# Second convolution of a fused network on four 32-column strips, and three whole-image passes on ScalarE

## The chip, the cores and the metric

The kernel runs on 1 core of one Trainium2 chip. The metric is the device time of one execution in microseconds. In this text PE is TensorE, DVE is VectorE, ACT is ScalarE, POOL is GpSimd and SP is SyncE, which only issues transfers; ACTq and SPq are the sequencers of ACT and SP while they issue one.

## What is computed

The input is 64 images of 16 channels of 128x128, float32. Four layers each add a function of the group-normalised image (8 groups of 2 channels) to the image:

```python
x = x + _L0_conv_ref(_gn(x), 5)      # Newton-Schulz inverse of each 128x128 channel, 5 iterations
x = x + _L1_conv_ref(_gn(x), L1_conv_weight_int8, L1_conv_scale_weight, L1_conv_bias)  # 8-bit 3x3
x = x + _L2_conv_ref(_gn(x), L2_conv_filter_w)
x = x + _L3_conv_ref(_gn(x), L3_conv_weight)   # 3x3 with circular borders
```

Layer 1 quantises its input with one step for the whole batch, `round(clip(x / scale_input, -127, 127))`. Layer 2 is a 5x5 convolution whose kernel is zero off its diagonal:

```python
kernel = filter_w[..., :, None] * jnp.eye(k, dtype=filter_w.dtype)   # k = 5, padding 2
```

So tap d reads the pixel d rows down and d columns to the right, d = -2 .. 2, and there are five taps and not 25.

## The kernel before

The program has two blocks. The first does the inverse of layer 0 for all images, and ends near 2272 us. The second does layers 1 to 3, and everything that the prediction speaks of lies there.

**Layout.** An image stands in SBUF as 128 partitions by 2048 elements. A partition is (row within a band of 8, channel), and the free dimension is (16 bands, 128 columns). Four bands make a chunk of 512 columns, one PSUM bank, so each layer has four chunks u = 0 .. 3. A convolution is a sum of matmuls of a 128x128 weight matrix (all rows and channels of a band to all rows and channels of a band) with a chunk shifted sideways, and one "halo" matmul with 96 partitions, for the input rows that lie in the neighbouring band. Those 6 rows x 16 channels are copied from the normalised image `xn` into the tile `xh` by six transfers of one row each, three issued by ACT (line 1184) and three by SP (line 1130). Layers 2 and 3 use float16 in two parts, a high part and the remainder, and so every weight matrix costs three products; layer 1 needs one.

**Normalisation.** For layers 2 and 3 DVE computes scale and mean in small columns (lines 1312 to 1320) and the scaled image F over 2048 elements (line 1322). ACT rounds F to float16 (`upper`, line 1202), POOL subtracts that from F (`lower`, line 1164, four instructions), and then the image counts as normalised (`normed`). For layer 1 DVE makes three passes over the image (`quantise`, lines 1243, 1246, 1248). In layer 3 ACT also copies the circular borders (`wrap`, lines 1192 to 1197), and then issues the halo transfers.

**Order.** The code is written out by hand as steps, and each engine has its own fixed order and waits on semaphores. PE's step s is layer 1 of image s, layer 2 of image s-1 and layer 3 of image s-2. The tiny matmuls `mean` and `var` of the next statistics stand between their chunks. The order on ACT in step s, with waits, is this:

```python
def step(s, h, odd):
    if there(s - 2):
        wrap(s - 2, odd)
        act.wait_ge(wrapped, 2 * s - 2)
        halos(3, s - 2, odd)
    if there(s):
        root(2, s)
        upper(2, s, odd)
    if there(s + 1):
        first(s + 1, h + odd, 1 - odd)
    if there(s):
        act.wait_ge(normed[2], s + 1)
        halos(2, s, odd)
    if there(s - 1):
        root(3, s - 1)
        upper(3, s - 1, 1 - odd)
```

`first` issues the halo transfers of layer 1 and adds the bias to the whole image (line 1214). `root` is the square root of a column (line 1207), which DVE waits for before its columns of lines 1312 to 1320.

Of the kernel before, what the change touches and what calls it, by code (L numbers as in the profile page):

```python
# [19 lines left out]
H = 128  # L20
C = 16
G = 8
CPG = C // G
RB = 8
NJ = H // RB
PW = H + 4
L = 2
# [6 lines left out]
WUP = 2.0 ** 14  # L34
# [7 lines left out]
def conv_net(nc, x, ident, gmat, gsel, w1, w1h, w2, w2h, w3, w3h, scale_w, bias, x1d, out):  # L42
# [32 lines left out]

    def images(step, first, last, turn):

        for i in range(first, last):
            step(i, i // turn, i % turn)

    keep = ExitStack()
    with keep:
# [19 lines left out]
        sws = persistent("sws", [H, 1])  # L102
        banks = [keep.enter_context(nc.psum_tensor(f"bank{n}", [H, 512], f32)) for n in range(8)]
# [3 lines left out]
        taps = (None, 3, 5, 3)  # L107
        kinds = (None, bf16, f16, f16)
# [3 lines left out]
        wt = [None] + [persistent(f"wt{l}", [H, parts[l], taps[l], H], kinds[l]) for l in (1, 2, 3)]  # L112
        wth = [None] + [persistent(f"wth{l}", [6 * C, parts[l], H], kinds[l]) for l in (1, 2, 3)]
        wf = [None] + [persistent(f"wf{l}", [H, taps[l], H]) for l in (1, 2, 3)]
        whf = [None] + [persistent(f"whf{l}", [6 * C, H]) for l in (1, 2, 3)]
# [9 lines left out]
        w_loaded = sem("w_loaded")  # L125
        w_top = sem("w_top")
# [11 lines left out]
        with mem:  # L138
# [103 lines left out]
            with nc.Block() as block:  # L242

                @block.sync
                def _(sp):
# [17 lines left out]
                    for l, body, rows in ((1, w1, w1h), (2, w2, w2h), (3, w3, w3h)):  # L263
                        sp.dma_start(wf[l][:, :, :], body).then_inc(w_loaded, 16)
                        sp.dma_start(whf[l][:, :], rows).then_inc(w_loaded, 16)
                    for i in range(A_FIRST):
                        step(i, i // SLOTS, i % SLOTS)
# [11 lines left out]
                def _(pool):  # L279
                    nc.gpsimd.memset(ones[:, :], 1.0).then_inc(ones_set, 1)  # L280
                    nc.gpsimd.memset(onesm[:, :], 1.0 / (2 * H)).then_inc(ones_set, 1)
                    nc.gpsimd.memset(onesv[:, :], 1.0 / (CPG * H * H)).then_inc(ones_set, 1)

# [144 lines left out]
                def _(act):  # L428
# [45 lines left out]
                    def upper_weights(l):  # L474

                        if l == 1:
                            act.wait_ge(w_loaded, 16 * 6)
                        else:
                            act.wait_ge(w_chain, 6 * (l - 1))
                        nc.scalar.activation(wt[l][:, 0, :, :], wf[l][:, :, :], ACT.Copy).then_inc(w_high, 1)  # L480
                        nc.scalar.activation(wth[l][:, 0, :], whf[l][:, :], ACT.Copy).then_inc(w_high, 1)
# [81 lines left out]
                def _(dve):  # L563
# [120 lines left out]
                    def weight_rows(l):  # L684

                        if l == 2:
                            dve.wait_ge(w_loaded, 16 * 6)
# [3 lines left out]
                    def weight_top(l):  # L691

                        w = wtop[l]
                        link = Link(dve, w_chain, 6 * (l - 2))
# [5 lines left out]
                    def weight_scale(l):  # L700

                        w = wtop[l]
                        link = Link(dve, w_chain, 6 * (l - 2) + 2)
                        dve.wait_ge(w_top_all, l - 1)
                        link.done(nc.vector.tensor_copy(w["s"][:, :], banks[7][:, H - 4 + l:H - 3 + l]))
                        link.wait()
                        link.done(nc.vector.reciprocal(w["i"][:, :], w["s"][:, :]))
                        link.wait()
                        link.done(nc.vector.tensor_scalar(wf[l][:, :, :], wf[l][:, :, :], w["i"][:, 0:1], WUP,
                                                          ALU.mult, ALU.mult))  # L710
                        link.done(nc.vector.tensor_scalar(whf[l][:, :], whf[l][:, :], w["i"][0:6 * C, 0:1], WUP,
# [4 lines left out]
                    def lower_weights(l):  # L716
                        dve.wait_ge(w_high, 2 * l)
                        nc.vector.tensor_tensor(wt[l][:, 1, :, :], wf[l][:, :, :], wt[l][:, 0, :, :],
                                                ALU.subtract).then_inc(w_split, 1)
                        nc.vector.tensor_tensor(wth[l][:, 1, :], whf[l][:, :], wth[l][:, 0, :],  # L720
                                                ALU.subtract).then_inc(w_split, 1)
# [124 lines left out]
                    link.wait()  # L846
                    dve.wait_ge(pads_zeroed, 6)
# [3 lines left out]
                def _(pe):  # L851
# [66 lines left out]
                    def weight_broadcast(l):  # L918
                        pe.wait_ge(w_chain, 6 * (l - 2) + 2)
# [579 lines left out]
```

## Time and profile before

| what | value |
|---|---|
| time, median of 3 runs | 4286.94 us (4285.88 to 4287.16) |
| span of the profiled execution | 4285.7 us, 1.2 us under the median |
| PE busy | 4194.6 us, 98% of the span |
| DVE busy | 3444.2 us, 80% |
| POOL busy | 2407.9 us, 56% |
| ACT busy | 2072.5 us, 48% |

The busy shares are means over both blocks. In the second block, which starts at about 2272 us, PE is at its limit and ACT and POOL are a quarter busy. ACT's busy time leaves out the time in which its sequencer issues transfers. Beginnings and ends of matmuls overlap in the trace, so the spacing of their starts says what one costs.

### The profile page before, as it was taken

What the parts mean: (1) busy time and instruction counts of PE and PEld (TensorE: products, weight loads), DVE (VectorE), ACT (ScalarE), POOL (GpSimd) and SP (SyncE); (2) the same over time, 40 slices, a digit from 0 to 9 for tenths busy, and PEclk for the clock granted to TensorE, in tenths of its full rate; (3) what the DMA queues carried; (4) which work ended last, traced back from release to release, by engine and by line L of the source; (5) the groups of instructions that cost most, each with busy time, mean ns of one, the idle gap of its engine ahead of it and who ended that gap; (6) DMA issues with size and microseconds to landing.
All of it is one profiled execution on the core that took longest, in us unless ns stands there. A gap on an engine that the chain in (4) does not pass through costs nothing. (4 is left out here: it accounts for less than half of the span.)

```text
span 4285.7 us, 81705 instructions
## 1 busy us (share of the span) xinstructions
PE 4194.6 (98%) x30409; PEld 3108.7 (73%) x30409; DVE 3444.2 (80%) x7393; ACT 2072.5 (48%) x4296; POOL 2407.9 (56%) x3149
## 2 busy tenths in 40 slices
PE   7999999999999999999996999999999999999998
PEld 7999999999999999999992444444444444444443
DVE  6888888888888888888876787878787888888784
ACT  5776777777777777777761222222222222222221
POOL 6888888888888888888871222222222222222221
PEclk9999999999999999999997999999999999999999
DMA  2221222222222222222214555555555555555553
GB/s 69 64 62 55 65 65 60 60 60 60 60 66 65 60 63 68 60 60 60 60 41 97 133 137 134 137 133 137 134 138 134 138 134 138 134 138 134 138 134 84
DMA packets 333657, 404.28 MB, mean 94 GB/s; under 512 B 23088, under 2 KB 286032, under 8 KB 316880
## 3 DMA queue, kind: packets, MB, share of 16 engines
q1 hardware_dynamic: 308688, 334.25, 30.8%
q10 hardware_dynamic: 24576, 64.79, 5.6%
q8 instruction: 246, 4.03, 0.4%
q14 instruction: 147, 1.20, 0.1%
HBM read 135.22 MB, written 134.22 MB: 63 GB/s over the span
## 5 line engine op out<-in xcount | busy, mean ns | idle before, releaser
L1392 PE MATMUL bank<-xn,wt 128*128 128x512 f16 (+1 forms) x6912 | 1661.6, 381 | 19.9 <-issue 10.7
L1164 POOL TENSOR_TENSOR xn<-F,xn 128x512 f16<-128x512 f32 x512 | 541.6, 1090 | 1453.2 <-ACT xn L1202 1453.2
L1392 PEld LDWEIGHTS bank<-xn,wt 128*128 128x128 f16 (+1 forms) x6912 | 672.9, 100 | 805.0 <-issue 21.9
L463 ACT ACTIVATE P<-bank 128x512 f32<-128x512 f32 x1024 | 606.8, 608 | 264.0 <-PE bank L962 154.5
L1266 DVE SCALAR_TENSOR_TENSOR x<-bank,wu,x 128x512 f32<-128x512 f32 x512 | 382.4, 747 | 313.7 <-PE bank L1399 306.6
L1202 ACT ACTIVATE xn<-F 128x2048 f16<-128x2048 f32 x128 | 244.9, 1913 | 603.3 <-DVE F L1322 603.3
L1399 PE MATMUL bank<-xh,wth 96*128 96x512 f16 (+1 forms) x1792 | 515.6, 380 | 12.1 <-DMA xh<-xn 12.1
L313 POOL TENSOR_TENSOR W<-W 128x512 f16<-128x512 f32 x256 | 290.3, 1166 | 145.7 <-ACT W L489 145.7
L1277 DVE BATCH_NORM_STATS2 bs<-x 128x6 f32<-128x512 f32 x512 | 355.6, 695 | 17.7
L569 DVE BATCH_NORM_STATS2 st<-X 128x6 f32<-128x256 f32 x1024 | 351.5, 411 | 5.8 <-DMA X<-in_x 5.7
L1399 PEld LDWEIGHTS bank<-xh,wth 96*128 96x128 f16 (+1 forms) x1792 | 174.2, 97 | 232.6 <-DMA xh<-xn 15.7
L358 POOL TENSOR_TENSOR S<-P 128x512 f32<-128x512 f32 x256 | 317.8, 1272 | 32.0 <-ACT P L463 31.6
L369 POOL TENSOR_TENSOR P<-P,idt 128x512 f32<-128x512 f32 x256 | 318.4, 1278 | 29.0 <-ACT P L463 28.8
L353 POOL TENSOR_TENSOR YX<-idt,YX 128x512 f32<-128x512 f32 x256 | 324.1, 1278 | 5.5 <-ACT YX L453 5.5
L498 ACT ACTIVATE W<-X,nb,r 128x256 f32<-128x256 f32 x512 | 259.4, 590 | 134.2 <-POOL nb L341 130.7
L1207 ACT ACTIVATE sd<-ve 128x1 f32<-128x1 f32 x128 | 26.1, 204 | 608.9 <-DVE ve L1303 603.0
L364 POOL TENSOR_TENSOR S<-S,P 128x512 f32<-128x512 f32 x256 | 318.1, 1274 | 0.0
L453 ACT ACTIVATE YX<-bank,cs 128x128 f32<-128x128 f32 x1024 | 277.7, 381 | 11.8 <-PE bank L894 3.5
L673 DVE SCALAR_TENSOR_TENSOR X<-bank,cout,X 128x128 f32<-128x128 f32 x1024 | 270.5, 344 | 12.9 <-PE bank L988 12.9
L607 DVE TENSOR_TENSOR P<-bank,idt 128x512 f32<-128x512 f32 x256 | 177.0, 692 | 109.0 <-PE bank L979 103.2
L929 PE MATMUL bank<-YX 128*128 128x128 f32 x2048 | 260.9, 276 | 0.0
L944 PE MATMUL bank<-P 128*128 128x128 f32 x2048 | 260.2, 277 | 0.0
(129 smaller groups left out, 7619.3 us busy)
## 6 DMA issues: line engine op xcount, KB each, us to landing
X<-in_x SPq DMA_DIRECT2D x64, 1024.0 KB, 4.8
x_scratch<-X SPq DMA_DIRECT2D x64, 1024.0 KB, 5.6
X<-x_scratch SPq DMA_DIRECT2D x64, 1024.0 KB, 8.8
out<-x SPq DMA_DIRECT2D x64, 1024.0 KB, 3.9
xh<-xn SPq DMA_DIRECT2D x384, 131.8 KB, 4.5
xh<-xn ACTq DMA_DIRECT2D x384, 131.8 KB, 5.4
xh<-xn SPq DMA_DIRECT2D x192, 65.9 KB, 3.2
xh<-xn ACTq DMA_DIRECT2D x192, 65.9 KB, 2.7
```

Source lines behind the costliest of these rows:

```text
L313: nc.gpsimd.tensor_tensor(W16[:, 1, at, :], W[:, at, :], W16[:, 0, at, :], ALU.subtract).then_inc(w_lower, 1)
L353: nc.gpsimd.tensor_tensor(e, eyes, e, ALU.subtract).then_inc(a_new, 1)
L358: nc.gpsimd.tensor_tensor(quad(S, q), quad(P1, q), quad(P2, q), ALU.add).then_inc(s_new, 1)
L364: nc.gpsimd.tensor_tensor(quad(S, q), quad(S, q), quad(P3, q), ALU.add).then_inc(q_new, 1)
L369: nc.gpsimd.tensor_tensor(quad(P2, q), quad(P2, q), eyes, ALU.add).then_inc(r_new, 1)
L463: nc.scalar.activation(into[:, 4 * q:4 * q + 4, :], banks[q][:, :].rearrange("p (m w) -> p m w", m=4), ACT.Copy).then_inc(sb, 1)
L569: ins = nc.vector.bn_stats((st0, st1)[k][:, g, :], group_of(X[slot], g))
L1164: ins = nc.gpsimd.tensor_tensor(padded(xn[l][odd], 1)[:, a + 1:a + 5, L:L + H], F[l][:, a:a + 4, :], padded(xn[l][odd], 0)[:, a + 1:a + 5, ...
L1266: nc.vector.scalar_tensor_tensor(out=dst, in0=bank, scalar=wtop[l]["u"][:, 0:1], in1=xs[l][odd][:, a:b, :], op0=ALU.mult, op1=ALU.add).the ...
L1277: nc.vector.bn_stats(bst_[l][:, u, :], xs[l][odd][:, 4 * u:4 * u + 4, :]).then_inc(gchain[l], 1)
L1392: nc.tensor.matmul(bank, wt[l][:, a, k, :], v, start=(k == a == b == 0), stop=False)
L1399: ins = nc.tensor.matmul(bank, wth[l][:, a, :], v, start=False, stop=(a, b) == products[-1])
```

## The change

Layer 2 is done in another form. The normalised halves of `xn` are copied into a new tile `xk`, each of the 8 rows of a band by one transfer, row r shifted by 7-r columns (`skew_row`). In `xk` all five taps of one output row lie in one column, so that one weight matrix, the sum of the five, serves where five shifts did. An output row o needs its own shift of the reading position, and so the 128 output partitions are worked in strips of 32 (two output rows of 16 channels), two matmuls to a strip (e = 0, 1: half of the matrix is zero in each). Strips 0 and 3 also need two matmuls for the neighbouring band. Each is 128 partitions in, 32 out, 512 columns. The 8 transfers are split between SP (even rows) and ACT (odd rows), and the first chunk of layer 2 waits for all 8.

Three whole-image passes move from DVE to ACT: the F passes of layers 2 and 3 (now the first line of `upper`), and the first pass of `quantise` (now `quotients`). DVE gets one more column instruction, `nb`, in `normalise`. `var(2)` moves from behind chunk 1 to behind chunk 2, and `mean(2)` from the middle of chunk 1 to its end.

```diff
+            def skew_row(eng, r, odd):
+                at, to = PW + L, PW + L + SK - r
+                eng.dma_start(xk[odd][C * r:C * r + C, :, to:to + RUN],
+                              xn[2][odd][C * r:C * r + C, :, at:at + RUN]).then_inc(skewed[odd], 16)
...
+                    def skew(n, odd):
+                        sp.wait_ge(normed[2], n + 1)
+                        sp.wait_ge(xk_zeroed, 2)
+                        for r in range(0, RB, 2):
+                            skew_row(sp, r, odd)
...
+                    for n in range(2):
+                        nc.gpsimd.memset(xk[n][:, :, :], 0.0).then_inc(xk_zeroed, 1)
...
+                    def quotients(n, h, odd):
+                        act.wait_ge(x1_in[odd], 16 * h + 16)
+                        need(act, normed[1], n)
+                        nc.scalar.activation(T[:, :, :], xs[1][odd][:, :, :], ACT.Identity, scale=acol[:, n:n + 1],
+                                             bias=ncol[:, n:n + 1]).then_inc(quotient, 1)
+
                     def upper(l, n, odd):
 
+                        act.wait_ge(scale_set[l], n + 1)
+                        need(act, normed[l], n)
+                        nc.scalar.activation(F[l][:, :, :], xs[l][odd][:, :, :], ACT.Identity, scale=cols[l]["r"][:, 0:1],
+                                             bias=cols[l]["nb"][:, 0:1]).then_inc(scaled_f[l], 1)
                         act.wait_ge(scaled_f[l], n + 1)
...
+                        if there(s + 1):
+                            quotients(s + 1, h + odd, 1 - odd)
                         if there(s):
                             root(2, s)
                             upper(2, s, odd)
...
-                            halos(2, s, odd)
+                            act.wait_ge(xk_zeroed, 2)
+                            for r in range(1, RB, 2):
+                                skew_row(act, r, odd)
...
-                        dve.wait_ge(x1_in[odd], 16 * h + 16)
-                        link = Link(dve, q_chain, 2 * n)
-                        link.done(nc.vector.tensor_scalar(T[:, :, :], xs[1][odd][:, :, :], mcol[:, bass.ds(n, 1)],
-                                                          acol[:, bass.ds(n, 1)], ALU.subtract, ALU.mult))
-                        link.wait()
+                        dve.wait_ge(quotient, n + 1)
+                        link = Link(dve, q_chain, n)
...
-                        nc.vector.tensor_scalar(F[l][:, :, :], xs[l][odd][:, :, :],
-                                                c["m"][:, 0:1], c["r"][:, 0:1], ALU.subtract,
-                                                ALU.mult).then_inc(scaled_f[l], 1)
+                        nc.vector.tensor_scalar(c["nb"][:, :], c["r"][:, :], c["m"][:, 0:1], -1.0, ALU.mult,
+                                                ALU.mult).then_inc(scale_set[l], 1)
...
+                    def diagonals(s, n, h, odd, u):
+
+                        bank = banks[(BPI + u) % B_RING]
+                        if u == 0:
+                            pe.wait_ge(skewed[odd], 16 * RB * (h + 1))
+                        bank_free(s, 2, u)
...
+                        for a, b in [(0, 0), (0, 1), (1, 0)]:
+                            for e in range(2):
+                                for q in range(4):
+                                    nc.tensor.matmul(bank[32 * q:32 * q + 32, :], wt[2][:, a, e, 32 * q:32 * q + 32],
+                                                     rows(b, 2 * q + e, 0), start=(a == b == e == 0),
+                                                     stop=(a == e == 1 and q in (1, 2)))
+                            for e in range(2):
+                                for q, back in ((0, -1), (3, 1)):
+                                    ins = nc.tensor.matmul(bank[32 * q:32 * q + 32, :], wth[2][:, a, e, 32 * q:32 * q + 32],
+                                                           rows(b, 2 * q + e, back), start=False, stop=(a == e == 1))
+                        ins.then_inc(conv_ps[2], 1)
```

In the first block the weights of layer 2 are summed over the taps (one reduction and smaller scalings on DVE, the splits in two instructions each), five more small transfers load them, and POOL clears three tiles at the start. A column `ncol`, minus mean times scale for each image, is made before the second block.

ACT's instructions of one step of the second block before the change, from the transfers of layer 2 (`halos(2)`) to `upper(2)` of the next step; `xh`, `xn` and `x` end in the number of their buffer, and `sd<-ve` is `root`:

```order
L1184 DMA xh_0<-xn_0 16x2x2108 [waits normed2]
L1184 DMA xh_0<-xn_0 16x2x2108 x2
L1207 ACTIVATE sd<-ve 128x1 [waits gvar_sb3]
L1202 ACTIVATE xn_1<-F 128x16x128 [waits scaled_f3]
L1192 ACTIVATE xn_1<-xn_1 128x2x16 [waits normed3]
L1194 ACTIVATE xn_1<-xn_1 128x2x16
L1196 ACTIVATE xn_1<-xn_1 128x2x132 [waits wrap_chain]
L1197 ACTIVATE xn_1<-xn_1 128x2x132
L1184 DMA xh_1<-xn_1 16x2x2108 [waits wrapped]
L1184 DMA xh_1<-xn_1 16x2x2108 x2
L1207 ACTIVATE sd<-ve 128x1 [waits gvar_sb2]
L1202 ACTIVATE xn_1<-F 128x16x128 [waits scaled_f2]
```

The same stretch after it:

```order
L1171 DMA xk<-xn_1 16x2x2108 [waits xk_zeroed,normed2]
L1171 DMA xk<-xn_1 16x2x2108 x3
L1284 ACTIVATE sd<-ve 128x1 [waits gvar_sb3]
L1276 ACTIVATE F<-x_0,nb,r 128x2048 [waits scale_set3]
L1279 ACTIVATE xn_0<-F 128x16x128 [waits scaled_f3]
L1258 ACTIVATE xn_0<-xn_0 128x2x16 [waits normed3]
L1260 ACTIVATE xn_0<-xn_0 128x2x16
L1262 ACTIVATE xn_0<-xn_0 128x2x132 [waits wrap_chain]
L1263 ACTIVATE xn_0<-xn_0 128x2x132
L1250 DMA xh_0<-xn_0 16x2x2108 [waits wrapped]
L1250 DMA xh_0<-xn_0 16x2x2108 x2
L1269 ACTIVATE T<-X,ncol,acol 128x2048 [waits normed1,x1_in1]
L1284 ACTIVATE sd<-ve 128x1 [waits gvar_sb2]
L1276 ACTIVATE F<-x_0,nb,r 128x2048 [waits normed2,scale_set2]
L1279 ACTIVATE xn_0<-F 128x16x128 [waits scaled_f2]
```

The fourth transfer, the two F passes and the T pass are new there. The T pass stands behind layer 3's transfers and ahead of `root(2)`, and the wait for `normed2` now holds four issues ahead of `root(3)`.

PE's instructions of layer 2, first chunk and the half of the second up to `mean`, before the change (line 1392 the taps, 1399 the halos, 1405 `mean`):

```order
L1392 MATMUL bank<-xn_1,wt 128x512 [waits evac3,normed2]
L1392 MATMUL bank<-xn_1,wt 128x512 x14
L1399 MATMUL bank<-xh_1,wth 128x512 [waits halo2_1]
L1399 MATMUL bank<-xh_1,wth 128x512 x2
L1392 MATMUL bank<-xn_1,wt 128x512 [waits evac3]
L1392 MATMUL bank<-xn_1,wt 128x512 x5
L1405 MATMUL bank<-s,gm 128x1 [waits gvar_sb2,bst_done2]
```

Chunk 0 and the first instruction of chunk 1 after it (line 1493 is the band itself, line 1498 the neighbouring band):

```order
L1493 MATMUL bank<-xk,wt 32x512 [waits evac3,halo2_1]
L1493 MATMUL bank<-xk,wt 32x512 x7
L1498 MATMUL bank<-xk,wth 32x512 x4
L1493 MATMUL bank<-xk,wt 32x512 x8
L1498 MATMUL bank<-xk,wth 32x512 x4
L1493 MATMUL bank<-xk,wt 32x512 x8
L1498 MATMUL bank<-xk,wth 32x512 x4
L1493 MATMUL bank<-xk,wt 32x512 [waits evac3]
```

The wait for the transfers (`halo2_1`) moved from the sixteenth instruction of the first chunk to its first, and a chunk went from 18 full-width matmuls to 36 of 32 output partitions.

## Rows read from the trace of the kernel before

**Rows 1.** The page: PE's busy share and granted clock in 40 slices.

```profile
PE   7999999999999999999996999999999999999998
...
PEclk9999999999999999999997999999999999999999
```

**Rows 2.** Stretch: length, busy us (instructions) of PE, PEld, DVE, ACT, POOL, clock, DMA share, GB/s.

```profile
3000.00:3500.00 500.00, 499.20 (x2360) 229.11 (x2359) 401.50 (x800) 121.65 (x146) 138.15 (x131) 1.00 0.57 136
```

**Rows 3.** PE in order of time, one step: start us, length us, instruction.

```profile
3003.67 0.82 PE L1392 MATMUL bank<-xn,wt 128*128 128x512 bf16 x3
...
3007.19 3.43 PE L1392 MATMUL bank<-xn,wt 128*128 128x512 f16 x15
3010.45 0.81 PE L1399 MATMUL bank<-xh,wth 96*128 96x512 f16 x3
...
3034.20 0.82 PE L1392 MATMUL bank<-xn,wt 128*128 128x512 bf16 x3
```

**Rows 4.** DVE in order of time, same step.

```profile
3017.13 1.33 DVE L1243 TENSOR_SCALAR T<-X,mcol,acol 128x2048 f32<-128x2048 f32 x1
3018.50 1.23 DVE L1246 TENSOR_SCALAR T<-T 128x2048 f32<-128x2048 f32 x1
...
3020.90 0.15 DVE L1312 RECIPROCAL ra<-sd 128x1 f32<-128x1 f32 x1
...
3021.86 1.35 DVE L1322 TENSOR_SCALAR F<-x,m,r 128x2048 f32<-128x2048 f32 x1
```

**Rows 5.** ACT in order of time, same step.

```profile
3013.13 0.35 ACT L1192 ACTIVATE xn<-xn 128x32 f16<-128x32 f16 x1 [4.34 <-POOL xn L1164]
...
3014.43 3.28 ACTq L1184 DMA_DIRECT2D xh<-xn  x3
3017.75 0.20 ACT L1207 ACTIVATE sd<-ve 128x1 f32<-128x1 f32 x1 [3.35 <-DVE ve L1303]
3023.24 1.91 ACT L1202 ACTIVATE xn<-F 128x2048 f16<-128x2048 f32 x1 [5.29 <-DVE F L1322]
3023.25 2.07 ACTq L1184 DMA_DIRECT2D xh<-xn  x3
...
3029.49 3.42 ACTq L1184 DMA_DIRECT2D xh<-xn  x3
3032.95 0.20 ACT L1207 ACTIVATE sd<-ve 128x1 f32<-128x1 f32 x1 [5.58 <-DVE ve L1303]
```

**Rows 6.** POOL in order of time, same step.

```profile
3008.87 4.23 POOL L1164 TENSOR_TENSOR xn<-F,xn 128x512 f16<-128x512 f32 x4 [9.92 <-ACT xn L1202]
3025.23 4.23 POOL L1164 TENSOR_TENSOR xn<-F,xn 128x512 f16<-128x512 f32 x4 [12.13 <-ACT xn L1202]
```

**Rows 7.** SP's issues in the same step.

```profile
3014.42 2.30 SPq L1130 DMA_DIRECT2D xh<-xn  x3
```

**Rows 8.** Transfers by kind in 3000:3500: KB each, median us to landing.

```profile
xh<-xn ACTq DMA_DIRECT2D x98, 131.8 KB, 5.4
```

**Rows 9.** ACT's groups by shape in 3000:3500: count, busy us, mean ns.

```profile
L1214 ACT ACTIVATE X<-X,bst 128x2048 f32<-128x2048 f32 x16 | 32.1, 2005 | 4.7 <-issue 4.5
```

**Rows 10.** ACT's groups by shape in 1000:1500.

```profile
L498 ACT ACTIVATE W<-X,nb,r 128x256 f32<-128x256 f32 x118 | 59.8, 591 | 30.3 <-POOL nb L341 30.3
L438 ACT ACTIVATE AD<-X,nm 128x256 f32<-128x256 f32 x112 | 46.2, 501 | 0.0
```

**Rows 11.** PE in order of time where the second block fills.

```profile
2325.99 0.58 PE L1405 MATMUL bank<-s,gm 128*128 128x1 f32 x2 [2.63 <-DVE s L1281]
...
2328.90 1.44 PE L1392 MATMUL bank<-xn,wt 128*128 128x512 bf16 x3
...
2333.39 0.82 PE L1392 MATMUL bank<-xn,wt 128*128 128x512 bf16 x3
```

**Rows 12.** POOL's clearing of a padded tile, 0:2270.

```profile
L286 POOL MEMSET xn<- 128x4752 f16 x4 | 16.2, 4062 | 0.0
```

**Rows 13.** POOL's first work in the second block.

```profile
2298.71 2.13 POOL L1164 TENSOR_TENSOR xn<-F,xn 128x512 f16<-128x512 f32 x2 [32.93 <-ACT xn L1202]
```

More of the change, by code:

```diff
@@ L102, in conv_net @@
         sws = persistent("sws", [H, 1])
+        ncol = persistent("ncol", [H, B])
         banks = [keep.enter_context(nc.psum_tensor(f"bank{n}", [H, 512], f32)) for n in range(8)]
@@ L262, in _ @@
                     load(2, 0, 2)
-                    for l, body, rows in ((1, w1, w1h), (2, w2, w2h), (3, w3, w3h)):
+                    for l, body in ((1, w1), (2, w2), (3, w3)):
                         sp.dma_start(wf[l][:, :, :], body).then_inc(w_loaded, 16)
+                    for l, rows in ((1, w1h), (3, w3h)):
                         sp.dma_start(whf[l][:, :], rows).then_inc(w_loaded, 16)
+                    sp.wait_ge(ones_set, 4)
+                    for k, (row, _, o) in enumerate(HALO2):
+                        r = row % RB
+                        sp.dma_start(whf[2][C * r:C * r + C, C * o:C * o + C],
+                                     w2h[C * k:C * k + C, C * o:C * o + C]).then_inc(w_loaded, 16)
                     for i in range(A_FIRST):
@@ L846, in _ @@
                     link.wait()
+                    link.done(nc.vector.scalar_tensor_tensor(out=ncol[:, :], in0=mcol[:, :], scalar=-1.0, in1=acol[:, :],
+                                                             op0=ALU.mult, op1=ALU.mult))
+                    link.wait()
                     dve.wait_ge(pads_zeroed, 6)
@@ L1071, in conv_net @@
             T = sb("T", [H, NJ, H])
-            xh = [None] + [[sb(f"xh{l}_{n}", [6 * C, parts[l], NJ * PW], kinds[l]) for n in range(2)] for l in (1, 2, 3)]
+            xh = [None] + [None if l == 2 else [sb(f"xh{l}_{n}", [6 * C, parts[l], NJ * PW], kinds[l]) for n in range(2)]
+                           for l in (1, 2, 3)]
+            xk = [sb(f"xk{n}", [H, 2, SFLAT], f16) for n in range(2)]
             F = [None, None] + [sb(f"F{l}", [H, NJ, H]) for l in (2, 3)]
@@ L1077, in conv_net @@
             PART = 512 // 2
-            cols = [None, None] + [{k: sb(f"{k}{l}", [H, 1]) for k in ("m", "s", "q", "ve", "sd", "ra", "rb", "r")}
+            cols = [None, None] + [{k: sb(f"{k}{l}", [H, 1]) for k in ("m", "s", "q", "ve", "sd", "ra", "rb", "r", "nb")}
                                    for l in (2, 3)]
@@ L1087, in conv_net @@
             q_chain = sem("q_chain")
+            quotient = sem("quotient")
+            scale_set = [None, None] + [sem(f"scale_set{l}") for l in (2, 3)]
             biased = sem("biased")
@@ L1419, in step @@
                             for u in range(BPI):
-                                conv(2, s, s - 1, h + odd - 1, 1 - odd, u,
-                                     (lambda: mean(2, s)) if u == 1 and there(s) else None)
+                                diagonals(s, s - 1, h + odd - 1, 1 - odd, u)
                                 if there(s) and u == 1:
+                                    mean(2, s)
+                                if there(s) and u == 2:
                                     var(2, s)
```

82 lines of the change are left out of this document (60 added, 22 removed).

## The prediction, made before the changed kernel ran

> **What bounds the kernel now.** I read the 40 slices first. PE is full and its clock is granted in full in the second block [rows 1]; a stretch inside it has PE busy 499.20 of 500 us, DVE 401.50, POOL 138.15 and ACT 121.65 [rows 2]. Then the order of time of PE gives the length of a step: layer 1's first chunk starts at 3003.67 and the next one at 3034.20, so a step is 30.53 us [rows 3]. The reader is to see there also what one full-width matmul costs: fifteen of them, 3007.19 to 3010.45, take 3.26 us, 0.2175 us each. A step has 16 of layer 1, 72 of layer 2 (18 to a chunk) and 48 of layer 3: 136 x 0.2175 = 29.58 us, and 0.95 us for the small matmuls and handovers. So PE sets the step, and everything else fits inside.
>
> Last I follow the other engines in the same step, because PE's work is what the change cuts. They hold a ring that comes back to itself once a step: transfers of layer 2, `root`, `upper` and `lower` of layer 3, its `wrap` and transfers, `root`, `upper` and `lower` of layer 2, and the transfers again. ACT executes it in this fixed order. Its pieces before, in us: three issues 3.46 (3029.49 to 3032.95) [rows 5]; `root` 0.25 with its handover; DVE's columns and F pass 0.96 + 1.38 + 0.05 (3020.90 to 3021.86, then 1.35) [rows 4]; `upper` 1.91 [rows 5]; `lower` 4.34, being 4.23, 0.08 ahead (3023.24 + 1.91 to 3025.23) and 0.03 behind (3013.10 to 3013.13) [rows 5, 6]; `wrap` 1.30 and three issues 3.32, 3013.13 to 3014.43 to 3017.75 [rows 5]; and then once more 0.25, 2.39, 1.91 and 4.34. That is 25.9 us, 4.6 less than the step, so today it costs nothing. The trace agrees with the slack: `root` is done at 3017.95 and DVE takes it up only at 3020.90, when its quantising passes are through [rows 4, 5].
>
> **PE after the change.** Layer 2 becomes 36 matmuls to a chunk, each 512 columns long and 32 wide. No row shows two matmuls on different strips, so I bound it. One after another they cost 36 x 0.2175 = 7.83 us, the step's PE work then being 13.92 (layers 1 and 3, 64 matmuls) + 31.32 + 0.95 = 46.2 us. If strips run side by side but each in order, a product is four rounds (e = 0, e = 1, and two of strips 0 and 3 alone), a chunk is 12 rounds, 2.61 us, and the step's PE work 13.92 + 10.44 + 0.95 = 25.3 us. Below that nothing is possible, because strips 0 and 3 have 12 matmuls each in a chunk. I take the side-by-side value, since the four write different partitions of one bank and only the last one signals; but any value up to 17 rounds changes nothing, as the next part shows.
>
> A page bears on this. The Trainium skill, TensorEngine Tiling (Array Packing), section Key Properties, says that tiles operate independently and that changing the tiling mode drains the array; TensorE: Matmul & The Clock Gate, section Measured speedup vs the span model, gives 3.07 times for four row tiles and 2.38 for three column tiles. By 3.07, an estimate from that page, a round costs 1.30 matmuls, a chunk 3.4 us and the step's PE work 28.5 us, which would still be a gain of 2 us a step if PE stayed the bound. No run here shows either yet.
>
> **DVE.** It loses 1.34 + 2 x 1.35 us a step and gains two columns of 0.15: of 401.50/500 x 30.53 = 24.5 us some 20.8 remain [rows 2, 4]. DVE isn't what was waited for, so this alone is worth nothing.
>
> **The ring after the change**, piece by piece:
> - Layer 2's issues on ACT go from three to four. Three took 3.46 us while SP issued three of its own, 1.15 each; four are 4.6 [rows 5]. The queue behind them holds `root(3)`.
> - `root` 0.25, unchanged.
> - Columns: 0.96, one more of 0.15, handovers 0.04: 1.15 [rows 4].
> - F pass on ACT: a 2048-element pass with a bias column takes 2.005 us [rows 9]; at 256 elements a scale column beside the bias column adds 0.591 - 0.501 = 0.09 [rows 10]. So 2.09.
> - `upper` 1.91 + 0.04 = 1.95, `lower` 4.34.
> - `wrap` 1.30 and layer 3's issues 3.32, unchanged.
> - T pass, the same form: 2.09. It stands behind those issues, and DVE can't quantise before it.
> - DVE's two remaining passes: 3018.50 to 3020.90, 2.40, handover 0.03 [rows 4]. Before, these lay beside ACT's `wrap` and issues. Now they come after them.
> - Columns 1.15 (`root(2)` is done meanwhile), F and `upper` 4.04, `lower` 4.34.
>
> The sum is 4.6 + 0.25 + 1.15 + 2.09 + 1.95 + 4.34 = 14.38; + 1.30 + 3.32 + 2.09 + 2.43 = 23.52; + 1.15 + 4.04 + 4.34 = 33.05 us. That is more than the old step, and PE doesn't occur in it. **The step becomes 33.05 us, 2.52 longer, with PE idle for about 7.7 of it.**
>
> A second ring goes through PE: start of layer 2 in PE, three chunks 7.83 and `mean` and `var` 0.4, columns and `root` 0.4, quantising 2.43, columns 1.15, F and `upper` 4.04, `lower` 4.34, then the last of four issues 3.45 after the first and 5.4 to land [rows 8]: 29.4 us. It is 3.6 us short of the first. The three chunks reach that only at 17 rounds each. All eight transfers are the same size as layer 2's six were (16 partitions by 2 by 2108 in the order); a late landing has these 3.6 us too.
>
> **The rest.** Start of the second block: `ncol` 0.25 and a T pass 2.09 for 1.34, +1 us. Clearing `xk` is two instructions like one of 4.06 us [rows 12], on a POOL that waits 32.93 us there [rows 13]; without that cover it would be 8 us once. In the first block DVE and ACT get a few instructions of under 1 us within a stretch that has room on ACT, and SP five issues at the start: +1 us, bounds 0 and 5. Layer 1's transfers, the load and the store keep their place or move past one more issue on SP (about 0.8 us, from 2.30 for three [rows 7]), each with over 10 us of cover.
>
> **Sum.** Steps 2 to 64 make 62 spacings: 62 x 2.52 = 156 us, and 2 us. On the profiled span 4285.7 + 158 = 4443.7; the median is 1.2 above the span, so 4445. Something is to be added where PE's idle time disturbs DVE, which I leave at 2: **4447 us**, 3.7% slower. Within 0.2%, some 9 us, a measurement can't tell it from no change.
>
> **Rivals.**
> 1. *The ring is shorter and the kernel is faster.* The price that is least certain is a transfer's issue on ACT. Where SP isn't issuing beside it, three cost 2.07 us, 0.69 each [rows 5]. If all seven of the ring cost that, it shrinks by 4 x 0.46 + 3 x 0.42 = 3.1 us to 29.9 and the time is 4287 - 62 x 0.6 = 4250. It decides from 2.5 us taken out. Against it: both queues are let go by the same semaphore, and layer 3's three keep their old neighbours [rows 5, 7]. Chance 8%, and 3% within 0.2%.
> 2. *PE stays the bound because strips overlap only in part, or its clock falls.* After a gap of 2.63 us in the filling stretch, three matmuls took 1.44 us instead of 0.82, for 4.5 us, 2328.90 to 2333.39 [rows 11]. The new step has some 7.7 us of gaps. Two or three such stretches cost 2 us each and fit in them; half the step at half speed would not: 25.3 + 12 = 37.3 us. Likewise 20 to 28 rounds a chunk give 32.3 to 39.2 us of PE work, and the second ring 35 to 40. With 34 to 40 us a step: 4500 to 4870. Chance 12%.
> 3. *Strips don't overlap at all*, or the clock stays at half: 46.2 us, 4285.7 + 62 x 15.7 = 5260. For it: nothing in the trace shows an overlap. The Trainium skill, TensorEngine Tiling (Array Packing), Key Properties, excludes it; the trace can't say. Chance 4%.
>
> **Numbers.** The ring as bound has 73%. Its own range comes from the four issues (3.0 at 0.75 each to 5.4) and from the 0.09 columns: a step of 31.5 to 34, 4345 to 4505. To leave out no more than 2 in 10, the range goes up into the second rival: 4345 to 4590. Faster 0.08, same 0.03, slower 0.89.
>
> **What would show it.** Right: a step of about 33 us in PE's order of time, PE busy about three quarters, waits of PE for the `xk` transfers and for DVE's sums; ACT's T pass starting right behind its three issues of layer 3, DVE's first quantising pass waiting for it some 4 us, and the `root` of layer 3 starting right behind four issues. POOL's two gaps in a step both end at an ACT pass. The first rival shows as issues of 0.7 us; the second as PE without gaps, or a granted clock below 1; the third as chunks of 7.8 us. The prediction is wrong if the T pass starts when ACT has been idle, or if DVE is ready later than it.

## The result, and the profile after

The changed kernel took **4456.61 us** (median, 4454.94 to 4459.2) beside 4287.05 us (4285.88 to 4288.18) for the kernel before: 1.0397 times as long, interval 1.0382 to 1.0411. The prediction was 4447 us, in a range of 4345 to 4590.

The page of the kernel after; under 2 the 40 slices, under 4 the chain that ended last.

```profile
span 4455.8 us, 91385 instructions
PE 4048.0 (91%) x35017; PEld 3008.5 (68%) x35017; DVE 3169.5 (71%) x7333; ACT 2465.2 (55%) x4490; POOL 2416.8 (54%) x3154
PE   7999999999999999999958888888888888888887
...
PEclk9999999999999999999978999999999999999998
...
ACT 16%; POOL 12%; ACTq 10%; DVE 7%; issue 2%; PE 2%; DMA 1%; POOLq 0%
```

PE's nines of the second block [rows 1] have become eights, and in the chain that ended last PE has 2% of the span; ACT, its queue, POOL and DVE have the second block.

The same stretch as in [rows 2], same columns:

```profile
3000.00:3500.00 500.00, 427.94 (x3261) 188.50 (x3260) 302.81 (x723) 206.46 (x181) 130.77 (x124) 0.92 0.60 133
```

PE is busy 427.94 us of 500 instead of 499.20 and the granted clock is 0.92 instead of 1.00: there are two losses, waiting, and a part of the time at the lower of the two levels, 1.2 GHz. PE is idle for 4.8 us of a step, where the prediction had 7.7: matmuls at half speed take up most of the difference. The length of a step, from one T pass to the fifty-third after it, is (4278.3 - 2527.6) / 53 = 33.03 us; before it was (4177.1 - 2528.7) / 54 = 30.53 us.

The chain in order of time for one step (start us, length us, what; L1171 are the `xk` issues, L1284 `root`, L1250 layer 3's issues):

```profile
3004.22 0.64 ACTq L1171
...
3008.54 0.21 ACT sd L1284
...
3010.00 2.10 ACT F L1276
...
3014.11 4.25 POOL xn L1228 x4
...
3019.67 0.60 ACTq L1250
...
3023.10 2.11 ACT T L1269
...
3025.23 1.24 DVE T L1325
...
3028.85 2.10 ACT F L1276
...
3032.96 4.24 POOL xn L1228 x4
3037.23 0.64 ACTq L1171
```

From issue to issue 3004.22 to 3037.23 is 33.01 us, and PE isn't in it. This is the first ring of the prediction, piece for piece.

PE in order of time in the same step (L1493 and L1498 are layer 2, L1505 and L1510 `mean` and `var`, L1469 layers 1 and 3):

```profile
3000.73 3.45 PE L1469 MATMUL bank<-xn,wt 128*128 128x512 f16 x9
...
3013.42 0.86 PE L1493 MATMUL bank<-xk,wt 128*32 128x512 f16 x8 [2.32 <-DMA xk<-xn]
...
3014.91 1.08 PE L1493 MATMUL bank<-xk,wt 128*32 128x512 f16 x6
...
3020.43 0.38 PE L1505 MATMUL bank<-s,gm 128*128 128x1 f32 x2
...
3023.48 0.38 PE L1510 MATMUL bank<-q,gm 128*128 128x1 f32 x2
3023.79 0.62 PE L1493 MATMUL bank<-xk,wt 128*32 128x512 f16 x8
...
3026.52 2.15 PE L1469 MATMUL bank<-xn,wt 128*128 128x512 f16 x9
```

The last chunk of layer 2 runs from 3023.79 to 3026.52: 36 matmuls in 2.73 us, so the four strips work side by side. The first chunks are another matter. Behind the wait of 2.32 us a group of six takes 1.08 us; at full clock even the eight from 3023.79 take only 0.62. From the start of layer 2 to `var` there are 10.06 us, where three chunks like the last, with 0.32 for the handover at `mean`, would be 8.5.

The wait of 2.32 us isn't the usual one. Of 36 such waits from 2600 to 3800, 32 are 3.8 to 4.6 us long (3.96 in the step before, 3.97 in the step after), one is 3.07 and three are 2.3 to 2.5. In this step PE had been at half speed already: behind a wait of 1.70 us for DVE's sums that ended at 2998.82, the last chunks of layer 3 slowed (the nine at 3000.73 take 3.45 us instead of 2.13), came to their end later and left less to wait.

### The profile page after: what moved, and what is told of

It reads as the page before. It is cut to its first block, busy times and chain, and to the rows that moved or that the text cites. A ratio compares the mean times of both kernels' runs of the same rounds, so it can differ in the third digit from the quotient of the medians.

```text
span 4455.8 us, 91385 instructions
## 1 busy us (share of the span) xinstructions
PE 4048.0 (91%) x35017; PEld 3008.5 (68%) x35017; DVE 3169.5 (71%) x7333; ACT 2465.2 (55%) x4490; POOL 2416.8 (54%) x3154
## 3 DMA queue, kind: packets, MB, share of 16 engines
q1 hardware_dynamic: 311840, 342.85, 31.8%
## 4 chain that ended last, share of the span: by engine, by line
ACT 16%; POOL 12%; ACTq 10%; DVE 7%; issue 2%; PE 2%; DMA 1%; POOLq 0%
POOL xn L1228 12%; ACTq L1171 6%; ACT F L1276 6%; ACT xn L1279 5%; ACTq L1250 4%; ACT T L1269 3%; DVE xn L1327 2%; DVE T L1325 2%; DMA xk<-xn 1%; PE bank L1493 1%; DVE nb L1400 1%; PE bank L1498 1%; ACT xn L1262 1%; DVE r L1398 0%; DVE rb L1392 0%
## 5 line engine op out<-in xcount | busy, mean ns | idle before, releaser
L1493 PE MATMUL bank<-xk,wt 128*32 128x512 f16 x6144 | 717.2, 441 | 260.9 <-DMA xk<-xn 260.9
L1469 PE MATMUL bank<-xn,wt 128*128 128x512 f16 (+1 forms) x3072 | 784.1, 387 | 26.1 <-DVE xn L1327 14.4
L1493 PEld LDWEIGHTS bank<-xk,wt 128*32 128x32 f16 x6144 | 280.2, 102 | 467.2 <-DMA xk<-xn 292.9
L1469 PEld LDWEIGHTS bank<-xn,wt 128*128 128x128 f16 (+1 forms) x3072 | 297.6, 101 | 394.2 <-issue 61.4
L1498 PE MATMUL bank<-xk,wth 128*32 128x512 f16 x3072 | 530.8, 425 | 0.0
L1276 ACT ACTIVATE F<-x,nb,r 128x2048 f32<-128x2048 f32 x128 | 268.0, 2094 | 306.0 <-DVE nb L1400 306.0
L1498 PEld LDWEIGHTS bank<-xk,wth 128*32 128x32 f16 x3072 | 179.5, 106 | 221.4 <-issue 85.8
L1476 PE MATMUL bank<-xh,wth 96*128 96x512 f16 (+1 forms) x1024 | 309.2, 383 | 14.0 <-DMA xh<-xn 14.0
L1284 ACT ACTIVATE sd<-ve 128x1 f32<-128x1 f32 x128 | 25.1, 196 | 466.6 <-issue 423.1
```

What stands on the lines that cost most here:

```text
L1276: nc.scalar.activation(F[l][:, :, :], xs[l][odd][:, :, :], ACT.Identity, scale=cols[l]["r"][:, 0:1], bias=cols[l]["nb"][:, 0:1]).then_inc( ...
L1469: nc.tensor.matmul(bank, wt[l][:, a, k, :], v, start=(k == a == b == 0), stop=False)
L1493: nc.tensor.matmul(bank[32 * q:32 * q + 32, :], wt[2][:, a, e, 32 * q:32 * q + 32], rows(b, 2 * q + e, 0), start=(a == b == e == 0), stop= ...
L1498: ins = nc.tensor.matmul(bank[32 * q:32 * q + 32, :], wth[2][:, a, e, 32 * q:32 * q + 32], rows(b, 2 * q + e, back), start=False, stop=(a ...
```

## The experiments

Ratios are to the kernel before, timed in turns with each run, with the 95% interval. A step is measured between T passes as above.

### Which half of the change costs the time

`t_on_dve` gives the T pass back to DVE:

```diff
-                        if there(s + 1):
-                            quotients(s + 1, h + odd, 1 - odd)
...
-                        dve.wait_ge(quotient, n + 1)
-                        link = Link(dve, q_chain, n)
+                        link.done(nc.vector.tensor_scalar(T[:, :, :], xs[1][odd][:, :, :], mcol[:, bass.ds(n, 1)],
+                                                          acol[:, bass.ds(n, 1)], ALU.subtract, ALU.mult))
```

> The changed kernel with the T pass back on DVE as its first of three quantising passes; the F passes stay on ACT. Ring theory: the first ring is 28.8 us as DVE's quantising lies beside ACT's issues again, the ring through PE grows by the third DVE pass to 30.7 to 31.2 us; time 4300 to 4340. Rival (PE and transfers): 4445 to 4465.

Measured: 4527.95 us, 1.0564 [1.0548, 1.0579], step 34.13 us. My expectation fell, and with the wrong sign: given the strips, the T pass on ACT *saves* 71 us. The chain of `t_on_dve` in one step shows why (same columns; the first and the last rows are the same transfer, one step apart):

```profile
2998.81 5.79 DMA xk<-xn
...
3004.64 1.05 PE bank L1493 x8
...
3016.02 0.16 DVE ve L1382
3016.18 1.26 DVE T L1322
...
3021.08 2.10 ACT F L1276
...
3025.20 4.24 POOL xn L1228 x4
3029.46 0.64 ACTq L1171
...
3032.93 5.63 DMA xk<-xn
```

This is the prediction's second ring, now the bound, and its price is 33.96 us: layer 2 in PE 11.38 (3004.64 to 3016.02; the prediction had 8.2), DVE 3.94 with the third pass, columns 1.12, F pass and `upper` 4.05, `lower` and handovers 4.33, issues 3.47, the transfer 5.63 and 0.04. Of the 3.15 us too much in PE, 2.46 come from half speed in chunks 0 and 1, behind a wait of 4.12 us: to `mean` at 3012.56 they take 7.92 us, where two of 2.73 would be 5.46.

`strips_only` is `t_on_dve` with the F passes on DVE too, so all three passes are where they were:

```diff
-                        nc.scalar.activation(F[l][:, :, :], xs[l][odd][:, :, :], ACT.Identity, scale=cols[l]["r"][:, 0:1],
-                                             bias=cols[l]["nb"][:, 0:1]).then_inc(scaled_f[l], 1)
...
+                        nc.vector.tensor_scalar(F[l][:, :, :], xs[l][odd][:, :, :],
+                                                c["m"][:, 0:1], c["r"][:, 0:1], ALU.subtract,
+                                                ALU.mult).then_inc(scaled_f[l], 1)
```

> The strips and their eight transfers alone, all three whole-image passes back on DVE. Ring theory: first ring 27 us, ring through PE 29.6 to 30.3 us; time 4235 to 4290, a little below the kernel before or the same. Rival (PE and transfers): 4445 or more, since the strips and transfers are all there.

Measured: 4319.6 us, 1.0074 [1.0059, 1.0089], step 30.78 us, clock 0.97 in 3000:4000. It missed its range by 30 us; the rival (strips alone make the kernel as slow as the whole change) fell too. Its chain in two steps (L1397 is the F pass on DVE, L1275 `upper`):

```profile
3000.53 0.83 PE bank L1491 x8
...
3014.15 1.36 DVE F L1397
...
3017.52 4.24 POOL xn L1228 x4
3021.78 0.64 ACTq L1171
...
3025.32 5.77 DMA xk<-xn
3031.14 0.94 PE bank L1491 x8
```

From layer 2 to layer 2, 3000.53 to 3031.14, the second ring is 30.61 us, about what PE's work alone was before: PE has 3.4 us less to do in a step (busy 880.58 us of 1000, which is 27.1 of 30.78, for 499.20 of 500 x 30.53 = 30.5), and nothing is gained.

`t_on_dve` differs from it only in the two F passes, and costs 208 us more. Of the 3.35 us between the two second rings shown, the F pass with its handover is 0.75 (2.13 for 1.38). PE is 2.57: 11.38 us from the start of layer 2 to `ve`, where `strips_only` takes 8.81 behind a wait of 1.81 us. So a longer ring costs more than what is put into it, once PE's wait in it is followed by half speed.

`passes_only` is the kernel before with the three passes on ACT, as in the diff of the change, and nothing else.

> The convolution of the kernel before (full-width matmuls, six halo transfers) with the three passes on ACT. Ring theory: the ring of 33.05 us less one issue of about 1.1, so 31.9 to 32.1 us; time 4370 to 4395, slower than before although nothing of PE changed. Rival (PE and transfers): PE's 30.5 us stay the bound, 4285 to 4295.

Measured: 4386.21 us, 1.0231 [1.0214, 1.0248], step (4246.3 - 2510.3) / 54 = 32.15 us, as expected by the ring. The stretch 3000:4000 of this kernel:

```profile
3000.00:4000.00 1000.00, 964.68 (x4478) 430.21 (x4477) 648.41 (x1498) 425.83 (x375) 263.39 (x250) 1.00 0.56 129
```

PE does the same work as before and is busy 96% at full clock; DVE lost work, and the kernel is 100 us slower. So the first ring is enough by itself: its chain in one step is the same as above with three issues for four, through ACT, DVE and POOL, and PE isn't in it. The step is 0.88 us shorter than with the strips; layer 2 has one issue fewer on ACT here, which the prediction priced at 1.15.

### Dose and relief of the first ring

`t_twice` makes ACT do one more whole-image pass ahead of the T pass, into a spare tile that nothing reads:

```diff
+                        nc.scalar.activation(Z[:, :, :], xs[1][odd][:, :, :], ACT.Identity, scale=acol[:, n:n + 1],
+                                             bias=ncol[:, n:n + 1])
                         nc.scalar.activation(T[:, :, :], xs[1][odd][:, :, :], ACT.Identity, scale=acol[:, n:n + 1],
```

> The changed kernel with the T pass made twice in its old place (first into a spare tile). A dose for the first ring. Ring theory: 2.09 us more in each of 62 steps, 4456 + 130 = 4586 (4570 to 4600). Rival (the ring through PE with its late transfers sets the changed kernel's step, as it does that of t_early): less than 60 us more.

Measured: 4595.34 us, 1.0718 [1.0702, 1.0734], step 35.33 us: 2.30 us more a step for a pass of 2.1.

`t_early` leaves the pass on ACT and only moves it ahead of `wrap` and layer 3's issues, into ACT's wait for `lower(3)`:

```diff
+                        if there(s + 1):
+                            quotients(s + 1, h + odd, 1 - odd)
                         if there(s - 2):
                             wrap(s - 2, odd)
...
-                        if there(s + 1):
-                            quotients(s + 1, h + odd, 1 - odd)
```

> The changed kernel with one thing moved: ACT makes the T pass (first quantising pass) at the start of its step, ahead of the borders of layer 3, where it waits for POOL anyway. Ring theory: the T pass of 2.09 us and DVE's two quantising passes of 2.43 us leave the ring of 33.05 us, which falls to 28.8; then the ring through PE, 29.4 to 29.9 us, is the longest, and the time is near 4240 (4220 to 4275), below the kernel before. Rival (PE's strips, its fallen clock of 0.92 and the late xk transfers set the step): nothing of PE's work or of the transfers changes, 4445 to 4465.

Measured: 4411.46 us, 1.0291 [1.0276, 1.0306], step 32.33 us. It is 45 us faster than the kernel after, but both theories missed it: the first ring is cut by `wrap`, issues and T pass, yet the step falls by only 0.70 us. Its PE in order of time:

```profile
2999.93 0.77 PE L1493 MATMUL bank<-xk,wt 128*32 128x512 f16 x8 [3.98 <-DMA xk<-xn]
...
3031.61 1.05 PE L1493 MATMUL bank<-xk,wt 128*32 128x512 f16 x8 [3.93 <-DMA xk<-xn]
```

Layer 2 starts at 2999.93 and again at 3031.61, 31.68 us later, each time let go by the transfers: the second ring binds here, and its chain in order of time goes through PE. Steps of some 31.8 and 33.0 us alternate for most of the block, which gives the mean of 32.33. The step before this one was 32.96, with 11.70 us from the start of layer 2 to the end of `var` for 10.45 here, as half speed lasted some 6 us there and 4 here. Once the first ring gives way, the second stands 0.7 us behind it, not 3.6.

### Does the second ring run through PE's speed?

`more_rounds` repeats one of the three products in layer 2, so that a chunk has 16 rounds (the output isn't the reference's, since one product is counted twice):

```diff
-                        for a, b in [(0, 0), (0, 1), (1, 0)]:
+                        for a, b in [(0, 0), (0, 1), (0, 1), (1, 0)]:
```

> The changed kernel with one of the three products of layer 2 made twice (48 matmuls to a chunk instead of 36, 16 rounds for 12), so its output isn't the reference's. As predicted, with 3.6 us of room in the second ring: no change, 4450 to 4465. If the second ring is as long as t_early shows (31.7 to 32.3 us, 0.7 to 1.3 us of room): three chunks of 0.9 us more, partly at half clock, take up the room and 1.5 to 2.5 us more a step, 4540 to 4620.

Measured: 4546.23 us, 1.0607 [1.059, 1.0625], step 34.32 us. The prediction's own statement, that up to 17 rounds change nothing, is wrong: 4 rounds more cost 90 us. Three chunks times four rounds at 0.2175 us are 2.6 us a step at full clock; 1.3 of them came through. A room of 0.7 would have let 1.9 through; the other 0.6 isn't explained (the granted clock in 3000:4000 is 0.95 for 0.92, and the waits for `xk` are some 3.5 us for 4.0).

`early_filled` is `t_early` with 18 matmuls that nobody reads, between the layer 1 chunks and the wait for the transfers. They fill the wait, into the bank that chunk 0 overwrites.

```diff
+                        bank_free(s, 2, u)
+                        if u == 0 and there(s):
+                            fill = padded(xn[1][1 - odd], 0)[:, 1:5, L:L + H]
+                            for _ in range(18):
+                                nc.tensor.matmul(bank[:, :], wt[1][:, 0, 0, :], fill, start=True, stop=True)
...
-                        bank_free(s, 2, u)
```

> t_early with 18 full-width matmuls of no use in PE's wait for the xk transfers, some 3.9 us, into the bank that chunk 0 overwrites. Theory A (the wait lowers PE's clock, and the three chunks behind it take 10.4 us instead of 8.4, within the second ring): the granted clock stays at 1.00, the step falls by about 2 us, time 4280 to 4330. Theory B (the strips or the transfers cost that time themselves): 4405 to 4420, or more by the added work.

Measured: 4298.22 us, 1.0027 [1.0017, 1.0038], step 30.40 us. Useless work made the kernel 113 us faster. `t_early` and then `early_filled` in 3000:4000:

```profile
3000.00:4000.00 1000.00, 873.36 (x6696) 385.19 (x6696) 619.34 (x1488) 422.34 (x373) 262.24 (x248) 0.92 0.61 137
```

```profile
3000.00:4000.00 1000.00, 985.46 (x7689) 448.06 (x7685) 668.64 (x1582) 449.79 (x395) 279.34 (x264) 1.00 0.63 146
```

The clock goes from 0.92 to 1.00 and the step loses 1.93 us. So the half-speed chunks were on the second ring. The fill also sits ahead of layer 2 and could have delayed it; it didn't cost what it gave.

`early_norm` is `t_early` with DVE's order changed: layer 2's columns ahead of the next image's quantising passes, which takes these (2.43 us) out of the second ring.

```diff
+                                if there(s):
+                                    normalise(2, s, odd)
                                 if there(s + 1):
                                     quantise(s + 1, h + odd, 1 - odd)
-                                if there(s):
-                                    normalise(2, s, odd)
```

> t_early with DVE making layer 2's scale columns ahead of its two quantising passes instead of behind them. Second-ring theory: 2.43 us leave the ring through PE, and the wait for xk shrinks, so the step falls from 32.3 to 29.3 to 29.9 us; time 4225 to 4265, below the kernel before. Rival (the first ring of 28.8 us was mis-sized too): above 4300.

Measured: **4212.04 us**, 0.9826 [0.9811, 0.984], step 29.07 us. It beats both kernels: 75 us under the kernel before and 245 under the one after, and also under its own expectation. PE still waits for `xk`, but only 1.42, 1.20 and 1.78 us in three steps from 3000 on, and the first eight matmuls behind each of these take 0.62 us, full speed; the clock is 0.99 in 3000:4000:

```profile
3000.00:4000.00 1000.00, 905.21 (x7376) 407.34 (x7375) 712.05 (x1645) 468.60 (x411) 292.05 (x276) 0.99 0.66 152
```

### What binds then

The chain of `early_norm` names a third ring:

```profile
3004.14 0.38 PE bank L1505 x2
...
3013.15 2.10 ACT F L1276
...
3017.26 4.25 POOL xn L1228 x4
...
3022.83 0.60 ACTq L1250
...
3027.44 0.21 DVE nb L1400
3027.65 1.15 DVE T L1325
...
3033.07 0.38 PE bank L1505 x2
```

`mean` of layer 3 at 3004.14, the rest of layer 3 in PE, F pass, `upper`, `lower`, `wrap` and issues of layer 3, `root` and columns of layer 2, DVE's two passes and two additions, and `mean` again at 3033.07: 28.93 us. I tried to shorten it. `short_rings` is `early_norm` with layer 2's F pass on DVE (0.75 us less a pass) and the clearing of `xk` later:

```diff
+                    pool.wait_ge(normed[1], 1)
...
-                        act.wait_ge(scale_set[l], n + 1)
-                        need(act, normed[l], n)
...
+                        if l == 3:
+                            act.wait_ge(scale_set[l], n + 1)
+                            need(act, normed[l], n)
+                            nc.scalar.activation(F[l][:, :, :], xs[l][odd][:, :, :], ACT.Identity,
```

> early_norm, with layer 2's F pass back on DVE (1.35 us for 2.09 and a handover) and xk cleared later. Both rings go through that pass: 0.7 us less in each of 62 steps and 5 us at the start, 4212 - 49 = 4163 (4150 to 4185). If DVE, which takes the pass in front of two chunks' additions, has become what PE waits for: 4190 or more.

`short_rings_sp` also gives all eight `xk` issues to SP:

```diff
-                        for r in range(0, RB, 2):
+                        for r in range(RB):
                             skew_row(sp, r, odd)
...
-                            for r in range(1, RB, 2):
-                                skew_row(act, r, odd)
```

> short_rings with all eight xk transfers issued by SP and none by ACT. The ring through ACT loses 4.3 us of issues; the last issue of SP comes at about 7 x 0.6 = 4.2 us instead of 3.5. If the ring through ACT is the longest: 60 us or more below short_rings. If the ring through PE is: 10 to 45 us above it.

Measured: 4305.22 us, 1.0041 [1.0026, 1.0056], step 30.84, and 4302.83 us, 1.0033 [1.002, 1.0046], step 30.75. Both missed: 93 us slower than `early_norm` for one pass moved back, and who issues the transfers makes no difference there. The F pass on DVE now stands between layer 2's columns and the quantising passes, which are on the third ring. PE of `short_rings` in order of time, layer 3:

```profile
3023.07 2.14 PE L1478 MATMUL bank<-xn,wt 128*128 128x512 f16 x9
3027.16 0.82 PE L1485 MATMUL bank<-xh,wth 96*128 96x512 f16 x3 [1.94 <-DMA xh<-xn]
...
3030.98 1.44 PE L1478 MATMUL bank<-xn,wt 128*128 128x512 f16 x3
```

A wait of 1.94 us, a second of 0.52, and then matmuls at half speed (1.44 us for three; at full speed 0.82). `fill_third_ring` puts 9 unused matmuls ahead of layer 3's first chunk, to take the wait away:

```diff
+                        if l == 3 and u == 0 and there(s):
+                            fill = padded(xn[1][odd], 0)[:, 1:5, L:L + H]
+                            for _ in range(9):
+                                nc.tensor.matmul(bank, wt[1][:, 0, 0, :], fill, start=True, stop=True)
```

> short_rings with 9 full-width matmuls of no use ahead of layer 3's first chunk, where PE waits 1.94 us for the xh transfers, into the bank that this chunk overwrites. Theory A (that wait lowers PE's clock in the middle of layer 3, on whose last chunk the ring through layer 3's scaling hangs): granted clock back to 0.99 or more, step from 30.8 to 29 us or less, time 4160 to 4210. Theory B (the third ring is that long at full clock as well): 4295 to 4310, or up to 4340 by the added work.

Measured: 4289.18 us, 1.0001 [0.9991, 1.001], step 30.57 us, clock 0.98 instead of 0.94. It falls between the two theories: 16 us come back. The traces say how the 93 us divide. Between two starts of DVE's first quantising pass with the granted clock at 1.00 lie 30.0 us in `short_rings` (3181.33 to 3211.38, and the steps like it) and in `fill_third_ring` (3141.62 to 3171.66), and 28.9 in `early_norm` (2998.65 to 3027.57). So at full clock the ring is 1.1 us longer, which is the F pass of 1.35 on DVE less the column `nb` of 0.21 that it replaces there: some 70 us over 62 steps. The remaining 23 or so go with the clock. The steps of `short_rings` at 0.89 take about 32 us, and in `fill_third_ring` steps of 31.7 at 0.95 are left, so the fill took only a part of it away.

### The start of the second block

`late_clear` is the kernel after with the clearing of `xk` held back until DVE's first two passes are through:

```diff
+                    pool.wait_ge(normed[1], 1)
```

> The changed kernel with POOL clearing xk only after DVE's first quantising is through. Theory A (two clearing instructions of POOL beside DVE's first two passes made those 3.02 and 5.07 us instead of 1.23 each): both passes are 1.23 to 1.3 us in the trace, and the time is 5 to 6 us lower, 4448 to 4453. Theory B (something else in the filling stretch slowed them): both stay long, time the same.

Measured: 4450.23 us, 1.038 [1.0363, 1.0397], 6.4 us less, with the same step of 33.01 us. POOL and DVE of the kernel after, then of `late_clear`, in order of time:

```profile
2273.17 9.19 POOL L1241 MEMSET xk<- 128x4784 f16 x2 [7.37 <-POOLq L254]
2275.32 3.02 DVE L1325 TENSOR_SCALAR T<-T 128x2048 f32<-128x2048 f32 x1 [2.65 <-ACT T L1269]
2278.37 5.07 DVE L1327 TENSOR_SCALAR xn<-T 128x2048 bf16<-128x2048 f32 x1
```

```profile
2275.67 1.23 DVE L1326 TENSOR_SCALAR T<-T 128x2048 f32<-128x2048 f32 x1 [2.65 <-ACT T L1270]
2276.93 1.23 DVE L1328 TENSOR_SCALAR xn<-T 128x2048 bf16<-128x2048 f32 x1
2278.22 8.11 POOL L1242 MEMSET xk<- 128x4784 f16 x2 [12.07 <-DVE xn L1328]
```

## Why the prediction was right, and where a term was off

**The bound moves off PE to a ring over ACT, POOL and DVE: right, and shown.** `passes_only` makes the ring bind with PE's work unchanged, `t_twice` lengthens it by what it adds. `t_early` takes the T pass and the issues out from under it and the kernel gets 45 us faster, though far less than the 180 to 235 expected, because the second ring is next. Two signs that the prediction named read otherwise: DVE's first quantising pass waited 1.18 us for the T pass and not some 4, since DVE had other work until shortly before; and the granted clock was below 1 (0.92), which the prediction had put down as a sign of its second rival. PE didn't set the step all the same: the chain of a step leaves it out, and in `passes_only` the same ring makes 32.15 us at a clock of 1.00.

**Its length: right.** 33.05 forecast, 33.01 in one step and 33.03 on average. The four issues took 4.32 us to `root` where 4.6 was priced, the F and T passes 2.10 where 2.09 was, `lower` with its handovers 4.34 as priced. The first rival, issues at 0.69 us each, fell: the four took 0.64, 1.26, 1.54 and 0.74 us. Its 0.69 came from layer 1's transfers, which are half as large (65.9 KB).

**PE's work: right at full clock.** With the half speed PE was busy 28.3 us a step (427.94 of 500) where 25.3 was priced. A chunk took 2.73 us for the 2.61 priced. The Trainium skill, TensorE: Matmul & The Clock Gate, Measured speedup vs the span model, led to an estimate of 3.4 us a chunk; the trace doesn't bear that out for four column strips of 512 columns. That strips run at the same time, as TensorEngine Tiling (Array Packing) of the Trainium skill says under Key Properties, the trace confirms. With that the third rival fell.

**The second ring, 29.4 us with 3.6 to spare: mis-sized.** It is the term that failed. In `t_on_dve` it is 33.96 us, of which the third pass is 1.3, and in `t_early` 31.68 in the step shown and 32.33 on average; nothing like 29.4. The part that was priced too low is PE's: from the start of layer 2 to the end of `var` the prediction had 8.2 us, and `t_early` takes 10.45 in the step shown, so nearly all of the 2.3 us missing there. The prediction had seen the cause, in its second rival: half speed behind a wait. But it placed those 2 us in PE's slack ("fit in them") where they belong to a ring that passes through PE. In the kernel after it lies under the first by about 0.7 us (33.03 less the 32.33 that `t_early` is left with), so the total came out right; the sentences that rested on the 3.6 us of room (17 rounds, a late landing) didn't, as `more_rounds` shows.

**The start of the second block: mis-sized.** The fourth T pass starts at 2360.82 where it was 2345.57 before, 15.2 us later. The forecast had 1 us for the first block and 1 for this start, and up to two of its 62 spacings fall here, so at most 7. The clearing of `xk` was costed at nothing, under POOL's idle time. POOL was idle, but DVE wasn't: the passes took 3.02 and 5.07 us instead of 1.23 each. The durations are those of taking turns, since two clearings of 4.06 [rows 12] and two passes of 1.23 from 2273.17 end at 2283.75, and the trace has 2283.44; POOL's two took 9.19 us for the 8.11 of `late_clear`. The Trainium skill, SBUF — State Buffer, section Who interferes with whom, says that GpSimd and DVE in one of its 2-port modes share a port pair that the first to issue holds for its whole instruction, and that a `tensor_scalar` can enter such a mode; the trace agrees with the turns, and can't show the port.

Two runs divide the 15.2 us. In `passes_only`, which has the same order on ACT and neither strips nor clearing, the fourth T pass starts at 2350.59, 5.0 us late. In `late_clear` it starts at 2355.45, so the clearing is 5.4 (the run's time is 6.4 us lower). Some 4.9 are left for the strips and their transfers: in the kernel after PE waits 6.77 and 7.66 us for them ahead of the first two images' layer 2. That remainder is by subtraction only.

**The sum.** 170.1 us of span are 15.2 at the start, 60 spacings at 2.53 (152.2) and 2.7 at the end. Forecast were 62 x 2.52 = 156 and 2, and 2 for the disturbance of DVE. Counted over the same 60 spacings the forecast has 151 for 152.2, and 9 for the 17.9 of the two ends. So the size of the step carries the result, and the ends are what it lacked.

## What to carry to other kernels

Before relieving the busiest engine, follow the waits through one step until they close, for every such ring, and price each with the change in; here three of them lay within 4 us of the old bound, and 75 us of gain or 170 of loss hung on the order of two calls in ACT's and DVE's streams. Where a ring passes through TensorE behind a wait like the 4 us here, price its first matmuls at half speed, and look whether the wait itself can go (an earlier release) before shortening the matmuls. Covering work by an idle engine needs a look at who else is running then, not only at that engine.

## What the runs showed that I had not expected

- PE ran at half speed (1.2 GHz) for 3 to 6 us of matmuls behind waits of some 4 us in the kernel after and in `t_early`, and behind 1.94 with another of 0.52 in `short_rings`. Behind 1.20, 1.42 and 1.78 us in `early_norm` it didn't; but in the kernel after it did so behind one of 1.70 (from 2999.73), so the length of the last wait alone doesn't tell. Filling the wait of `t_early` with 18 matmuls that nobody reads took that kernel from 4411 to 4298 us.
- A small 128x1 matmul between two layer 2 chunks costs 0.31 us until the next chunk starts (3023.48 to 3023.79); between full-width chunks it was 0.14 (3004.67 to 3004.81).
- Two clearings on POOL and two passes on DVE have the durations of taking turns: DVE's second pass took 5.07 us instead of 1.23, and both were 1.23 when the clearing came later.
